# First attention of a four-layer latent transformer: another order and other buffers at its beginning

## The reference, cut to what matters

```python
# x: (2, 512, 256) latents; ctx: (2, 1024, 256); 16 heads of 64
c = layer_norm(ctx) * ln_ctx_g + ln_ctx_b
l = layer_norm(layer_norm(x)) * ln_lat_g + ln_lat_b   # as the kernel has it
q = l @ Wq                                            # (2, 16, 512, 64)
k, v = split(c @ Wkv)                                 # (2, 16, 1024, 64)
k = k * cos + rotate_half(k) * sin                    # rope, keys only
p = exp(clip(q @ k.T / 8, -11, 11)); p = p / sum(p)
x = x + (p @ v) @ Wo + bo
```

## Time and profile before

| | before |
|---|---|
| median of 3 runs | 2766.04 us (2760.65 to 2767.31) |
| profiled execution | 2766.01 us |
| its span, first to last instruction | 2764.3 us |
| TensorE busy | 2154.2 us (78%) |
| VectorE busy | 1379.5 us (50%) |
| ScalarE, GpSimd busy | 757.4 us (27%), 700.7 us (25%) |
| mean granted TensorE clock | 0.876 |

### The profile page before, as it was taken

The page is one execution under the profiler, slowest core; times in us unless marked ns, Lnnn a source line. Parts: engine busy times, 40 slices in busy tenths (PEclk is TensorE's granted clock), DMA queues, the critical chain, the costliest instruction groups (busy, mean ns, idle before and its releaser), DMA issues.

```text
span 2764.3 us, 34540 instructions
## 1 busy us (share of the span) xinstructions
PE 2154.2 (78%) x13832; PEld 1500.8 (54%) x13832; DVE 1379.5 (50%) x2156; ACT 757.4 (27%) x1164; POOL 700.7 (25%) x757
## 2 busy tenths in 40 slices
PE   2789898659958888885985787399678888469994
PEld 2445444248944444443883554299534544368883
DVE  4688888733136667675314543222465564412123
ACT  2444444212122333331112322000124445211111
POOL 3212121033320010001223221355411010154443
PEclk8899999869978999997996777599879999689997
DMA  4011000048920000001571000389300000078883
GB/s 142 16 30 32 23 26 18 8 158 284 316 98 8 11 15 10 8 8 41 182 254 37 16 12 5 118 311 328 131 12 18 10 11 3 22 267 294 294 293 103
DMA packets 96559, 274.66 MB, mean 99 GB/s; under 512 B 14128, under 2 KB 44592, under 8 KB 96016
## 3 DMA queue, kind: packets, MB, share of 16 engines
q0 software_dynamic: 45168, 206.99, 21.6%
q1 hardware_dynamic: 51232, 65.46, 7.6%
HBM read 239.50 MB, written 20.32 MB: 94 GB/s over the span
## 4 chain that ended last, share of the span: by engine, by line
PE 54%; DVE 20%; issue 10%; DMA 6%; ACT 5%; POOL 4%; another core or an unknown queue 0%; SPq 0%; DVEq 0%; POOLq 0%; ACTq 0%
PE psum L1976 11%; PE psum L277 9%; PE psum L1999 7%; PE psum L742 5%; PE psum L722 5%; DVE plain L888 5%; DVE plain L1513 3%; PE psum L1343 3%; PE psum L1316 2%; DMA plain<-sorted_x 2%; DMA plain<-in_l_en,plain 2%; PE psum L1360 2%; ACT plain L1028 2%; DVE plain L861 2%; PE psum L315 1%
## 5 line engine op out<-in xcount | busy, mean ns | idle before, releaser
L1976 PE MATMUL psum<-plain 128*128 128x128 f32 x3904 | 492.4, 279 | 10.4 <-DMA plain<-in_l_shared 8.6
L1976 PEld LDWEIGHTS psum<-plain 128*128 128x128 f32 x3904 | 484.8, 195 | 22.5 <-issue 9.7
L277 PE MATMUL psum<-split 128*128 128x256 f32 (+1 forms) x1728 | 379.9, 373 | 71.1 <-DVE split L350 9.8
L277 PEld LDWEIGHTS psum<-split 128*128 128x128 f32 x1728 | 286.8, 210 | 202.0 <-issue 115.9
L2100 POOL DMA_INDIRECT plain<-in_l_ffn,plain x274 | 259.9, 949 | 401.6 <-PE psum L1999 379.4
L1999 PE MATMUL psum<-plain 128*128 128x256 f32 x1160 | 303.8, 385 | 33.2 <-DVE plain L2065 30.6
L1028 ACT ACTIVATE plain<-psum 128x1024 f32<-128x1024 f32 x224 | 227.4, 1023 | 359.7 <-PE psum L742 246.1
L888 DVE TENSOR_TENSOR plain<-plain 128x1024 f32<-128x1024 f32 x200 | 265.6, 1328 | 12.4 <-ACT plain L1028 9.4
L722 PE MATMUL psum<-plain 128*64 128x512 f32 x896 | 241.8, 640 | 32.3 <-DVE plain L895 27.4
L742 PE MATMUL psum<-split 64*128 64x512 f32 x1536 | 237.0, 432 | 37.0 <-DVE plain L861 30.0
L1056 POOL TENSOR_TENSOR plain<-plain 128x512 f32<-128x512 f32 x48 | 67.7, 1410 | 673.1 <-DMA plain<-plain 669.9
(11 more groups left out here) (176 smaller groups left out, 2278.9 us busy)
## 6 DMA issues: line engine op xcount, KB each, us to landing
plain<-plain SPq DMA_DIRECT2D x192, 64.0 KB
plain<-sorted_x SPq DMA_DIRECT2D x76, 128.0 KB
sorted_y<-plain SPq DMA_DIRECT2D x76, 128.0 KB
plain<-in_l_w SPq DMA_DIRECT2D x20, 256.0 KB
plain<-in_l_ffn,plain POOLq DMA_INDIRECT x274
plain<-in_ctx SPq DMA_DIRECT2D x8, 512.0 KB, 5.9
plain<-in_l_wo SPq DMA_DIRECT2D x28, 128.0 KB, 2.0
plain<-in_l_tab SPq DMA_DIRECT2D x3, 1024.0 KB
```

The source lines that it names most:

```text
L277: m = t.e.matmul(out, lhs[x], rhs[y], start=(first and n == 0), stop=(last and n == 2), skip_group_check=skip)
L1976: m = t.e.matmul(K.bank(b)[:, 256 * z + P * f:256 * z + P * f + P], ws[:, f, c0:c0 + 128], xt[:, k, :], start=(f == 0 and k == 0 and z == ...
```

## The change

The order at the beginning of the first attention is written out anew. Context blocks 0 and 1 get one buffer of eight tiles (`STAGE8[0]`), blocks 2 and 3 another (`STAGE8[1]`), and each engine norms both blocks before it turns either. The second buffer also takes the normed latents (`XL`), and the turns use temporaries of their own (`TMP2`) in place of the buffers that rope writes. The engines' first preparation (`first`) puts the statistics of x between the scaling and the turns of the context, and the latents' second norm beside the key projections; the splits of the keys come behind the latents' turns, the second pair's weights last. GpSimd makes all latents' powers, then rope, then the bias. Blocks 2 and 3 are no longer worked on ahead of step 0: they are four pieces of side work at the start of step 0, with weights 0.2, 0.2, 1.0 and 1.0. All four values groups of batch 1 go into step 1. SyncE issues the context first, x ahead of the tables, and blocks 2 and 3 when the latents' last transposes are done. The second attention keeps its order.

```diff
-        self.STAGE2 = [view(5120 + 1024 * i, 1024, "p (t d) -> p t d", d=D) for i in range(2)]
+        self.STAGE8 = [view(o, 2048, "p (t d) -> p t d", d=D) for o in (5120, 22748)]
+        self.XL = self.STAGE8[1]
+        self.TMP2 = [view(24796 + 512 * i, 512) for i in range(2)]
...
+def vector_pair(v, K, bt):
+    for h in range(2):
+        yield
+        vector_pair_stats(v, K, bt, h)
+        vector_pair_scaled(v, K, bt, h)
+    for h in range(2):
+        yield
+        vector_turn(v, K, K.C64, 2 * bt + h, K.gain["ctx"], K.TMP2)
...
+def tensor_pair(t, K, bt, ring):
+    for h in range(2):
+        yield
+    for h in range(2):
+        yield
+        t.wait_ge("normed", t.next("normed", 4))
+        tensor_turn(t, K, K.STAGE8[bt], 4 * h, ring, True)
+        K.at["context", 0, 2 * bt + h] = t.made["turned"]
...
@@ Plan64
+            if n == 0 and not own:
+                weights = [0.2, 0.2, 1.0, 1.0] + weights
...
+        if m == 1 and not self.own:
+
+            return ([], []) if n == 1 else ([(1, 0), (1, 1)], [(1, x) for x in range(2, self.units)])
...
-def side64(n, A, divide, prepare, output, tail):
+def side64(n, A, divide, prepare, output, tail, context):
...
+    elif not A.own:
+
+        yield from context
+        yield
...
@@ vector_attention64
+    def first():
+
+        wsplit(0)
+        wvsplit(0)
+        v.wait_ge("x", 16)
+        vector_late_stats(v, K)
+        for h in range(2):
+            vector_turn(v, K, K.C64, h, K.gain["ctx"], K.TMP2)
+        v.wait_ge("tab", 16)
+        sin = K.TB[:, 1024:2048]
+        v.e.tensor_scalar(sin, sin, K.SGN, None, ALU.mult).then_inc(*v.up("tables"))
+        vector_late_scaled(v, K, K.XL, True)
+        keys(0, 0)
+        keys(0, 1)
+        vector_late_turn(v, K, K.XL, K.gain["lat"], K.TMP2)
+        split(0, 0)
+        split(0, 1)
+        query(0)
+        wsplit(1)
...
-    run(prepare(0), 1000)
-    if L == 0:
-        run(vector_context(v, K, K.gain["ctx"], [2, 3], K.STAGE2, K.K32), 1000)
+        run(prepare(0), 1000)
+    else:
+        first()
+        context = skip_first(vector_pair(v, K, 1))
...
@@ scalar_attention64
+    def first():
+
+        wsplit(0)
+        wvsplit(0)
+        for h in range(2):
+            scalar_turn(s, K, K.C64, h, K.gain["ctx"], K.TMP2)
+        keys(0, 0)
+        keys(0, 1)
+        for x in range(A.units):
+            values(0, x)
+        scalar_late(s, K, K.gain["lat"], K.TMP2)
+        split(0, 0)
+        split(0, 1)
+        query(0)
+        wsplit(1)
...
@@ gpsimd_attention64
+        gpsimd_late_stats(g, K, True)
+        n = g.seen["normed"] - 8
+        rope(0, 0)
+        rope(0, 1)
+        gpsimd_bias(g, K, n)
+        context = skip_first(gpsimd_pair(g, K, 1))
...
@@ sync_attention64
-        run(sync_context(y, K, 0, [2, 3], K.STAGE2), 1000)
+        y.wait_ge("turned", K.at.get(("late", L), 0))
+        sync_pair(y, K, 1)
...
@@ vector_program
-    run(vector_context(v, K, K.gain["ctx"], [0, 1], K.STAGE2, K.K32), 1000)
-    v.wait_ge("tab", 16)
...
+    for h in range(2):
+        vector_pair_stats(v, K, 0, h)
+    for h in range(2):
+        vector_pair_scaled(v, K, 0, h)
...
@@ sync_program
+    sync_pair(y, K, 0)
     sync_load64(y, K, 0, 0)
     sync_load_values64(y, K, 0, 0)
     sync_load_out64(y, K, 0, 0)
-    run(sync_context(y, K, 0, [0, 1], K.STAGE2), 1000)
+    y.e.dma_start(K.X, T["x"].rearrange("b (t p) d -> p (b t) d", p=P)).then_inc(*y.dma("x"))
     y.e.dma_start(K.TB, T["l0_tab"]).then_inc(*y.dma("tab"))
     y.e.dma_start(K.BIAS, T["bc"][:, 0:256]).then_inc(*y.dma("bias"))
-    y.e.dma_start(K.X, T["x"].rearrange("b (t p) d -> p (b t) d", p=P)).then_inc(*y.dma("x"))
```

More of the change, by code:

```diff
@@ L420, in gpsimd_late, with gpsimd_late_stats @@
+def gpsimd_late_stats(g, K, gain):
     for h in range(2):
@@ L422, in gpsimd_late, with gpsimd_bias, tensor_late @@
     for h in range(2):
-        n = g.next("normed", 4)
+        g.next("normed", 4)
         if gain:
             gpsimd_stats(g, K, 4 * h, 4 * h + 4)
[L426 to L431, removed]
     if gain:
         g.next("normed", 8)
-def tensor_late(t, K, gain, ring):
+def gpsimd_bias(g, K, n):
+    g.wait_ge("bias", g.next("bias", 16))
+    g.wait_ge("normed", n)
+    for i in range(NT):
+        g.before_next()
+        g.e.tensor_tensor(K.X[:, i, :], K.X[:, i, :], K.BIAS, ALU.add).then_inc(*g.up("biased"))
+def tensor_late(t, K, xn, gain, ring):
     n = t.next("normed", 8)
@@ L668, in late @@
     def late():
-        tensor_late(t, K, True, RB)
+        tensor_late(t, K, K.XN if own else K.XL, True, RB)
         K.at["late", L] = t.made["turned"]
@@ L788, in tensor_attention64 @@
     run(prepare(0), 1000)
-    if L == 0:
-        run(tensor_context(t, K, 0, [2, 3], K.STAGE2, RB), 1000)
+    context = iter(()) if own else skip_first(tensor_pair(t, K, 1, RB))
     for n in range(A.n):
-        side = side64(n, A, divide, prepare, output, tail)
+        side = side64(n, A, divide, prepare, output, tail, context)
         attend(n, side)
@@ L817, in keys @@
             v.wait_ge("rope_add", (L, n - 1, c))
-        if n == 1:
+        if n == 1 and own:
             v.wait_ge("turned", K.at.get(("late", L), 0))
@@ L832, in late @@
         vector_before(v, K, L)
-        vector_late(v, K, K.gain["l" if own else "lat"])
+        vector_late(v, K, K.gain["l"])
     def query(n):
@@ L984, in late @@
         s.wait_ge("k_lo", (L, 0, 1))
-        scalar_late(s, K, K.gain["l" if own else "lat"])
+        scalar_late(s, K, K.gain["l"], K.K32)
     def query(n):
@@ L1033, in tail @@
         scalar_half(s, K, 0)
[L1035 to L1040, removed]
+    def first():
+        wsplit(0)
+        wvsplit(0)
+        for h in range(2):
+            scalar_turn(s, K, K.C64, h, K.gain["ctx"], K.TMP2)
[7 more added lines that the diff above has]
+        query(0)
+        wsplit(1)
+    context = iter(())
+    if own:
+        wsplit(0)
+        wvsplit(0)
+        wsplit(1)
+        run(prepare(0), 1000)
+    else:
+        first()
+        context = skip_first(scalar_pair(s, K, 1))
     for n in range(A.n):
-        side = side64(n, A, nothing, prepare, nothing, tail)
+        side = side64(n, A, nothing, prepare, nothing, tail, context)
         attend(n, side)
@@ L1097, in tail @@
         gpsimd_half(g, K, 0)
-    run(prepare(0), 1000)
-    if L == 0:
-        run(gpsimd_context(g, K, [2, 3]), 1000)
+    context = iter(())
+    if own:
+        run(prepare(0), 1000)
+    else:
+        gpsimd_late_stats(g, K, True)
+        n = g.seen["normed"] - 8
+        rope(0, 0)
+        rope(0, 1)
+        gpsimd_bias(g, K, n)
+        context = skip_first(gpsimd_pair(g, K, 1))
     for n in range(A.n):
-        side = side64(n, A, nothing, prepare, nothing, tail)
+        side = side64(n, A, nothing, prepare, nothing, tail, context)
         attend(n, side)
@@ L1604, in late @@
     def late():
[L1605 removed]
+        scalar_late(s, K, None, K.K32)
     def shift(n):
@@ L2338, in tensor_program @@
     ring = Ring([4, 5, 6, 7])
-    run(tensor_context(t, K, 0, [0, 1], K.STAGE2, ring), 1000)
+    run(tensor_pair(t, K, 0, ring), 1000)
     for L in range(4):
```

63 lines of the change are left out of this document (45 added, 18 removed).

## The result

| | before | after |
|---|---|---|
| median | 2766.14 us (4 runs) | 2742.92 us (2738.05 to 2746.17, 4 runs) |
| profiled execution, span | 2766.01, 2764.3 us | 2738.05, 2736.2 us |
| ratio of the fast runs | | 0.9913, 95% interval [0.9887, 0.9939] |

A forecast was written before the change was run, and what follows sets the result against it. The beginning was taken as bound by latency, a chain going round the engines with none full. 2766.0 - 37.3 (start) + 12.5 (step 0) + 1.5 (step 1) = 2742.7, said as 2743 us, range 2735 to 2750.

The forecast's parts named there:

- The start: Everything before the first attention scores: they start at 52.5 us against 89.8, 37.3 earlier, bounds 49.5 and 58.
- the table load: ScalarE's load of 1.28 us at the beginning, on the path before, now lies under the wait for the context.
- the third gain's wait: ScalarE, context turns of blocks 0 and 1: two buffers only, so it waits for VectorE's first remainder, near 19.6 us.
- the scaling beside the bias: Latents' second half on VectorE: scaling takes 2.73 us beside GpSimd's bias sums, against 1.38 alone.
- Step 0: First attention step, now holding the other batch's context: 37.8 us against 25.3, 12.5 longer.
- 19.6 + 3.0: Step 0 behind the context's transposes: rest of the normal step 19.6 us, plus 3.0 with the second key projection's chain late.
- Rival 1: The context really hides in step 0, which grows by only 4 us: total 2734; chance 0.17.
- Step 1: Second attention step: two more values groups, 3.0 us of TensorE, lengthen it by 0 to 3.0, taken as 1.5.
- The sum: Whole kernel: 2766.0 - 37.3 + 12.5 + 1.5 = 2742.7 us, said as 2743.
- (2): The start shrinks less: first scores at 60 instead of 52.5 us, total 2750; chance 0.15.
- (3): TensorE's waits in step 0 leave it at 1.2 GHz: 32 us over steps 0 and 1, total 2775; chance 0.03.
- Rival 4: Context load comes late and holds step 0, or later clock shifts by 1%: win shrinks to within 8 us; chance 0.04.

The follow-up runs named there:

- split_pieces: Changed kernel, but step 0's first context piece makes both blocks' statistics and the second both scalings, instead of one block each; 2730.83 us.
- ctx_ahead: Changed kernel, but context blocks 2 and 3 are normed and turned side by side ahead of step 0 instead of within it; 2741.49 us, 0.9916.
- values_ahead: Changed kernel, but step 1 makes its four values groups ahead of the query instead of two behind it; 2738.63 us, 0.9912.
- blocks_in_turn: Changed kernel, but VectorE takes block 0 through statistics, scaling and turn before block 1, both before the weights and x; 2753.22 us, 0.9961.
- changed_again: Changed kernel run once more without an edit, beside three others on one chip; 2739.78 us, 0.9924.

## Why the prediction was right, and where it was not

**The start.** Forecast 52.5, measured 50.8. The working holds at each station: VectorE's first statistics 7.4, measured 6.46; turns done 23.2, measured 21.95; cosine products 31.9, measured 30.2; late transposes 35.7, measured 34.1; from there 12.4 forecast, 12.2 measured; query 4.3 and 4.4. Of the 1.7 us of difference 0.9 was made by the first load, which landed that much earlier than my value; the rest came in small amounts by the end of the cosine products. One reading of the prediction was wrong without a cost: the table load does not lie under the wait for the context, which is there at 6.46; it starts at 8.62, when the weights have landed, and lies beside VectorE's statistics and scaling. Both costs that I named, the third gain's wait and the scaling beside the bias, were shown by taking each away: 2.3 and 2.1 us. The scaling took 3.22 where 2.73 was counted.

**Step 0.** Forecast 37.8, measured 39.2. First clip at 3.5 (forecast 3.2, end), scalings' end 12.8 (12.6), transposes 14.8 (14.6), turns 17.6 (17.2). From TensorE's second pair of tiles to the end 24.4 us, forecast 23.2. Of the 1.4 us that the forecast is short, 1.2 therefore lie behind the context's pieces, in the stretch for which the prediction took 19.6 + 3.0 and an allowance for the clock. split_pieces gave 3.4 us by taking out two waits of 1.55, which the prediction counted among the serial ones. Rival 1, that the context hides under step 0, was refuted by ctx_ahead: on balance nothing of it is hidden.

**Step 1, the step that failed.** "They fill its 3.6 idle us or push the step: between 0 and 3.0, I take 1.5." Measured 5.2, above the upper bound; its length, 33.9, is also outside the 29 to 32 named as a sign. The error was not in the matmuls. I priced the two groups as work of TensorE and did not ask who waits for their last one: ScalarE does, for a buffer, in a piece that the change now puts ahead of two of them. values_ahead, with the same work, took 4.6 of the 5.2 back. An edit that changes an order was costed as if it changed an amount.

**The sum.** By step 2 the forecast gain was 23.3 and the trace's is 19.9; the medians differ by 23.2. That the number came out to a tenth is luck: the start was 1.7 better, steps 0 and 1 together 5.1 worse, and behind step 2 the two profiled executions part without any change in their instructions. TensorE's first scores of some later steps run wholly or in part at 1.2 GHz in one execution and at 2.4 in the other (granted clock from 255 to 259 us: 0.64 before, 1.00 after). Before, steps 6, 7 and 10:

```profile
255.65 2.59 PE L742 MATMUL psum<-split 64*128 64x512 f32 x12
...
284.93 2.51 PE L742 MATMUL psum<-split 64*128 64x512 f32 x12
...
370.62 2.35 PE L742 MATMUL psum<-split 64*128 64x512 f32 x12
```

after, one step in the same stretch:

```profile
235.87 2.93 PE L836 MATMUL psum<-split 64*128 64x512 f32 x12
```

Twelve at 2.4 GHz take 1.66. From the start of step 6 to that of step 10 the kernel before takes 115.0 us with TensorE busy for 104.0, the changed one 111.8 with 101.2: the gain has grown from 19.8 to 23.0. The slow scores within this stretch differ by only 0.5 us (0.9 and 0.9 before, 1.3 after, against 1.66); the rest is not traced. To the end the gain in the profile becomes 28. The interval of 17 to 31 holds both 19.9 and 23.3, so that the true effect outside the first two steps stays open; none is needed.

**Rivals 2, 3, 4.** The start did not come late (2). Of the clock (3) I had written that below 0.9 in steps 0 and 1 together it would be this rival: the windows have 0.73 and 0.94, together 0.83, so the sign was given. But the price was a fraction of its 32 us. Windows of the changed kernel's step 0:

```profile
50.76:58.90 8.14, 2.93 (x12) 1.93 (x12) 4.21 (x15) 1.02 (x1) 1.27 (x2) 0.50 0.13 32
58.90:65.53 6.63, 3.87 (x17) 3.14 (x18) 4.90 (x16) 4.36 (x6) 1.26 (x2) 0.50 0.00 0
81.00:87.00 6.00, 6.00 (x23) 2.25 (x20) 5.46 (x6) 2.21 (x4) 3.08 (x2) 0.72 0.09 22
```

TensorE comes into the step at 1.2 GHz (the query projection at 46.33 takes 2.93 as well), stays there through its two waits of 5.28 and 2.69 us for VectorE and the work around them, and is there again for a part of 81 to 87 us. What it did there took 6.0 us longer than the same at 2.4 GHz: the two pairs of score tiles 2.93 instead of 1.66 each, the two blocks' transposes 1.97 instead of 1.04 each, a group of weighted values 3.13 instead of 1.94 (at 81.43), the query projection 2.09 instead of 1.65 (at 84.49). In step 0 before, it was 1.1 us. Only part of this reaches the end of the step: in values_ahead and blocks_in_turn the first pair took 1.66, and step 0 lasted 38.2 and 38.0 against 38.9 in changed_again. How much of step 0's miss is the clock no run shows. A mean clock over a window with waits is no measure of time lost. Rival 4 did not happen: the loads issued at 43.55 held nothing, VectorE's statistics began right behind the clip at 54.2.

## What to carry to other kernels

In a stage where no engine is full, write down one round over the engines and fill each wait with instructions of another, independent block that stand behind it in the same queue. Taking this filling away from the first two blocks and x cost 10 us here; moving two blocks' rounds into step 0 gave nothing. Look first for independent work that is queued behind a long chain: x behind rope was worth 14 us by the timelines. When an edit moves work behind something, look up every wait on its last result, and on its buffer, in every engine, before pricing it by its busy time. Compare stage boundaries in the traces when the effect sought is smaller than the spread of the total.

## What the runs showed of the hardware

Four scalings on VectorE that take 1.38 us alone took 3.43 beside GpSimd's rope sums and 3.22 beside its bias sums, 2.3 to 2.5 times as long; before they took 2.73 in a similar place. With the bias sums moved away the second took 1.38 again. With them moved, step 0's first clip took 1.24 beside them instead of 0.69. In the kernel before, ScalarE's table load of 1.28 us stood between the first transposes and the first gain (15.00 to 16.30); in the changed kernel ScalarE's first work is the rounding of the weights, the load stands ahead of that (8.62), and ScalarE still waits 1.62 us for the first transposes.
